# A fused AdaLN block on one core: the experts' second layer as three float32r products, gate rows gathered by GpSimd, all first-layer results on ScalarE

## What is computed

```python
mod = (_silu(L0_c) @ L0_wmod).reshape(L0_c.shape[0], 6, 1, -1)
...
h = _layernorm(x) * (1 + ca) + sa
x = x + ga * attention(h)
h = _layernorm(x) * (1 + cb) + sb
# the experts, on xf = h as 4096 rows of 256
score = softmax(xf @ Wg + bg);  gate, idx = max, argmax        # 16 experts
pos = rank of the token in its expert;  keep = pos < 256
buf[idx, pos] = xf                                             # 16 x 256 rows
hid = relu(einsum('ecd,edh->ech', buf, W1) + b1)               # 256 -> 1024
y = einsum('ech,ehd->ecd', hid, W2) + b2                       # 1024 -> 256
out = where(keep, y[idx, pos] * gate, 0)
x = x + gb * out
```

## Time and profile before

| | us |
|---|---|
| median of 3 runs | 1287.49 (1286.31 to 1287.84) |
| profiled execution, whole | 1285.58 |
| its span, first to last instruction | 1283.7 |
| mean granted TensorE clock | 0.979 of full |

### The profile page before, as it was taken

How to read it: one execution, slowest core, us unless ns; L and a number is a source line. 1 busy time by engine, 2 the same in 40 slices (tenths; PEclk the granted TensorE clock), 3 DMA queues, 4 the chain that set the end, 5 groups by cost and what they waited for, 6 DMA issues and landing times.

```text
span 1283.7 us, 23573 instructions
## 1 busy us (share of the span) xinstructions
PE 1193.8 (93%) x7518; PEld 846.1 (66%) x7518; DVE 860.7 (67%) x2159; ACT 599.7 (47%) x1419; POOL 342.5 (27%) x529
## 2 busy tenths in 40 slices
PE   5799999999999999999999999999998939999995
PEld 2555555656666666666666666666665829999994
DVE  6677777676676766766667666666664546777673
ACT  2465665555555555555555545555444023332320
POOL 3222121213232232323232312224333330111112
PEclk8999999999999999999999999999998959999998
DMA  4520221112121222212121222134425844676730
GB/s 152 203 109 26 107 86 62 37 58 75 59 74 57 74 70 66 84 63 70 65 74 60 73 78 71 59 99 157 162 76 201 305 150 143 200 251 208 239 129 19
DMA packets 100244, 139.66 MB, mean 109 GB/s; under 512 B 9917, under 2 KB 71487, under 8 KB 100033
## 3 DMA queue, kind: packets, MB, share of 16 engines
q1 hardware_dynamic: 91600, 113.55, 26.9%
q10 hardware_dynamic: 4464, 16.25, 3.2%
q0 software_dynamic: 4096, 8.82, 1.8%
HBM read 94.50 MB, written 48.00 MB: 111 GB/s over the span
## 4 chain that ended last, share of the span: by engine, by line
PE 70%; issue 11%; ACT 9%; DVE 6%; POOL 2%; DMA 2%; DVEq 0%; SPq 0%; ACTq 0%; POOLq 0%
PE SC L824 17%; PE Z L844 15%; PE Z L1001 9%; ACT E L1042 8%; PE SC L974 7%; PE XA L880 7%; PE XA L796 3%; PE XB L806 3%; PE XA L806 3%; PE XB L796 2%; PE SC L760 1%; PE XB L866 1%; DVE SC L1344 1%; DVE nm L1344 1%; DMA xln<-in_x 1%
## 5 line engine op out<-in xcount | busy, mean ns | idle before, releaser
L1042 ACT ACTIVATE E<-SC,nm 128x512 f32<-128x512 f32 (+7 forms) x512 | 375.0, 740 | 407.7 <-DVE nm L1344 407.7
L1344 DVE CUSTOM_DVE_ANT_0 SC<-SC,mask 128x512 f32<-128x512 f32 (+7 forms) x512 | 375.9, 786 | 160.3 <-PE SC L824 160.1
L824 PE MATMUL SC<-XQ,XK 64*128 64x512 f32 (+3 forms) x2304 | 264.6, 359 | 32.8 <-ACT E L1042 29.5
L824 PEld LDWEIGHTS SC<-XQ,XK 64*128 64x128 f32 x2304 | 185.5, 186 | 130.6 <-issue 103.3
L844 PE MATMUL Z<-E,vs 128*64 128x512 f32 (+3 forms) x1536 | 270.5, 494 | 0.3 <-DVE vs L1320 0.3
L844 PEld LDWEIGHTS Z<-E,vs 128*64 128x64 f32 x1536 | 99.9, 137 | 135.7 <-issue 124.7
L1001 PE MATMUL Z<-W,hh 128*128 128x256 f32 x512 | 113.2, 379 | 2.3 <-issue 2.3
L1001 PEld LDWEIGHTS Z<-W,hh 128*128 128x128 f32 x512 | 96.0, 190 | 15.1 <-issue 2.7
L1042 ACT ACTIVATION_READ_ACCUMULATOR E<-SC,nm 128x1 f32 x512 | 101.4, 198 | 0.0
L880 PE MATMUL XA<-woT,zt 128*128 128x256 f32 x384 | 89.3, 385 | 0.0
L1133 ACT ACTIVATE hh<-SC,b1t 128x256 f32<-128x256 f32 x64 | 26.9, 471 | 121.1 <-PE SC L974 121.1
(11 more groups left out here) (247 smaller groups left out, 1987.0 us busy)
## 6 DMA issues: line engine op xcount, KB each, us to landing
W<-in_w SPq DMA_DIRECT2D x32, 1024.0 KB, 8.2
z_s<-zs ACTq DMA_DIRECT2D x31, 512.0 KB, 2.6
zt<-z_s SPq DMA_DIRECT2D x24, 512.0 KB, 3.8
W<-in_wqk SPq DMA_DIRECT2D x33, 257.0 KB, 2.7
slots_s<-zt SPq DMA_DIRECT2D x16, 520.0 KB, 3.9
xb<-slots_s SPq DMA_DIRECT2D x16, 520.0 KB, 3.8
Wv<-in_wv SPq DMA_DIRECT2D x17, 256.0 KB, 2.6
xln<-in_x SPq DMA_DIRECT2D x24, 128.0 KB, 2.5
```

The costliest lines, as they stand in the source:

```text
L824: last = pe.matmul(SC[h][:, at:at + z - a], XK[rows, ap, kp, lo:lo + P], XQ[rows, ap, qp, a:z], start=(t == 0), stop=(t == 2))
L1042: act.activation(E[:, h, EOFF[kb]:EOFF[kb + 1]], SC[h][:, at:at + S - lo], ACT.Exp, bias=nm[:, h, kb:kb + 1], scale=-1.0, accum_out=rs[:, ...
L1344: dve.tensor_tensor_reduce(SC[h][:, at:at + S - lo], SC[h][:, at:at + S - lo], mask[:, 0:S - lo], 1.0, BIG, ALU.add, ALU.min, nm[:, h, kb: ...
```

## The change

Five things change, all but the table of memory in the expert stage.

1. The second layer is split like the first. ScalarE's `second_high` copies `W2` to `W2h`, VectorE's `second_low` subtracts to `W2l`; `hh` is copied to `hhh` by ScalarE and subtracted to `hhl` by VectorE. TensorE multiplies three pairs, 48 float32r matmuls in place of 16 float32 ones.
2. ScalarE takes all four groups of the first layer's results; `hh` has one buffer, and ScalarE waits for the last `hhl` (`hh_lo`) before it fills it again.
3. The eight gate operations on VectorE go. GpSimd casts a row number from a new column `MODROW` of the slot rows and gathers the modulation rows for the 256 tokens from DRAM (`mod_s`) into `grow` by two indirect DMAs. VectorE sums the four gate columns (`gsum`) and multiplies by both in one fused operation per half.
4. `W2` has two buffers of its own and a load of its own (`load_second_weights`), which in SyncE's queue waits for `w2_hi` and `w2_lo` of the expert two before.
5. The tiles `modB`, `woT` and `zt` lie lower, so that `hh`, `hhh` and `hhl` can take their place; the new column is filled by a few memsets; some semaphores are merged.

```diff
+MODROW = GATE + B
...
+        top[0] = place["modB"]
+        hh = sb("hh", [P, NM, CAP])
+        hhh = sb("hhh", [P, 2, NM, CAP], F32R)
+        hhl = sb("hhl", [P, 2, NM, CAP], F32R)
+        assert top[0] == place["E"]
...
-        W2 = sb("W2", [P, NW, NM, D])
+        W2 = sb("W2", [P, 2, NM, D])
+        W2h = sb("W2h", [P, 2, NM, D], F32R)
...
+        def load_second_weights(eng, e, k):
+
+            eng.dma_start(W2[:, k % 2, :, :], w2_d[e].rearrange("(m p) n -> p m n", p=P)).then_inc(w2_in[k % 2], 16)
+
         def load_expert(eng, e, k):
 
-            eng.dma_start(W2[:, k, :, :], w2_d[e].rearrange("(m p) n -> p m n", p=P)).then_inc(we_in[k], 16)
...
+                sp.wait_ge(w2_hi, k - 1)
+                sp.wait_ge(w2_lo, k - 1)
+                load_second_weights(sp, k, k)
...
+                    sp.wait_ge(w2_hi, e - 1)
+                    settle(sp, sp_passed)
+                    sp.wait_ge(w2_lo, e - 1)
+                    settle(sp, sp_passed)
+                    load_second_weights(sp, e, k)
...
-                pe.wait_ge(we_in[k], 48 * (j + 1))
                 pe.wait_ge(y_done, e + ONE)
-                for m in range(4):
-                    pe.wait_ge(hid_done[m], e + 1)
+                pe.wait_ge(w2_hi, e + 1)
+                pe.wait_ge(w2_lo, e + 1)
+                pe.wait_ge(hh_hi, e + 1)
+                pe.wait_ge(hh_lo, e + 1)
                 for i in range(2):
                     for m in range(NM):
-                        last = pe.matmul(yps[k % 2][:, i * D:(i + 1) * D], hh[:, k % 2, m, i * P:(i + 1) * P], W2[:, k, m, :],
-                                         start=(m == 0), stop=(m == NM - 1))
+                        for n, (x, w) in enumerate(((hhh, W2h), (hhh, W2l), (hhl, W2h))):
+                            last = pe.matmul(yps[k % 2][:, i * D:(i + 1) * D], x[:, k % 2, m, i * P:(i + 1) * P], w[:, k % 2, m, :],
+                                             start=(m == 0 and n == 0), stop=(m == NM - 1 and n == 2))
                 last.then_inc(y_mm, 1)
...
-            def hidden(e, j, k):
-                act.wait_ge(we_in[k], 48 * (j + 1))
+            def second_high(e, j, k):
+                act.wait_ge(w2_in[k % 2], 16 * (NW // 2 * j + k // 2 + 1))
                 if not isinstance(e, int) or e > 1:
                     act.wait_ge(y_mm, e - 1 + ONE)
-                for m in (0, 2):
+                act.activation(W2h[:, k % 2, :, :], W2[:, k % 2, :, :], ACT.Copy).then_inc(w2_hi, 1)
+
+            def hidden(e, j, k):
+                act.wait_ge(we_in[k], 32 * (j + 1))
+                if not isinstance(e, int) or e > 0:
+                    act.wait_ge(hh_lo, e)
+                if not isinstance(e, int) or e > 1:
+                    act.wait_ge(y_mm, e - 1 + ONE)
+                for m in range(4):
                     act.wait_ge(hid_mm[m], e + 1)
                     for half in range(2):
-                        last = act.activation(hh[:, k % 2, 2 * m + half, :], hid[m][:, half * CAP:(half + 1) * CAP], ACT.Relu,
+                        last = act.activation(hh[:, 2 * m + half, :], hid[m][:, half * CAP:(half + 1) * CAP], ACT.Relu,
                                               bias=b1t[:, k, 2 * m + half:2 * m + half + 1])
                     last.then_inc(hid_done[m], 1)
+                for m in range(4):
+                    act.wait_ge(hid_done[m], e + 1)
+                act.activation(hhh[:, k % 2, :, :], hh[:, :, :], ACT.Copy).then_inc(hh_hi, 1)
 
             def expert(j, k):
                 e = NW * j + k
                 if not isinstance(e, int) or e + 1 < NE:
                     hidden(e + 1, j + (k + 1) // NW, (k + 1) % NW)
+                    second_high(e + 1, j + (k + 1) // NW, (k + 1) % NW)
...
             weights_high(1, 0, 1)
+            second_high(0, 0, 0)
...
-            def hidden(e, j, k):
-                dve.wait_ge(we_in[k], 48 * (j + 1))
+            def second_low(e, k):
+                dve.wait_ge(w2_hi, e + 1)
                 if not isinstance(e, int) or e > 1:
                     dve.wait_ge(y_mm, e - 1 + ONE)
-                for m in (1, 3):
-                    dve.wait_ge(hid_mm[m], e + 1)
-                    for half in range(2):
-                        last = dve.tensor_scalar(hh[:, k % 2, 2 * m + half, :], hid[m][:, half * CAP:(half + 1) * CAP],
-                                                 b1t[:, k, 2 * m + half:2 * m + half + 1], 0.0, ALU.add, ALU.max)
-                    last.then_inc(hid_done[m], 1)
-
-            FIN = 2 * B + 2
+                dve.tensor_tensor(W2l[:, k % 2, :, :], W2[:, k % 2, :, :], W2h[:, k % 2, :, :].bitcast(F32), ALU.subtract).then_inc(w2_lo, 1)
+
+            def hidden(e, k):
+                dve.wait_ge(hh_hi, e + 1)
+                if not isinstance(e, int) or e > 1:
+                    dve.wait_ge(y_mm, e - 1 + ONE)
+                dve.tensor_tensor(hhl[:, k % 2, :, :], hh[:, :, :], hhh[:, k % 2, :, :].bitcast(F32), ALU.subtract).then_inc(hh_lo, 1)
+
+            FIN = 4
 
             def expert(j, k):
                 e = NW * j + k
                 if not isinstance(e, int) or e + 1 < NE:
-                    hidden(e + 1, j + (k + 1) // NW, (k + 1) % NW)
+                    hidden(e + 1, (k + 1) % NW)
+                    second_low(e + 1, (k + 1) % NW)
                 if not isinstance(e, int) or e + 2 < NE:
                     rows_low(e + 2, (k + 2) % NW)
                     weights_low(e + 2, (k + 2) % NW)
 
                 dve.wait_ge(xb_in[k], 16 * (j + 1))
-                for b in range(B):
-                    for i in range(2):
-                        col = xb[:, k, i, GATE + b:GATE + b + 1]
-                        if b == 0:
-                            if not isinstance(e, int) or e > 0:
-                                dve.wait_ge(fin, FIN * e)
-                            last = dve.tensor_scalar(grow[:, i, :], modB[:, b, GB, :], col, None, ALU.mult)
-                        else:
-                            dve.wait_ge(fin, FIN * e + 2 * (b - 1) + i + 1)
-                            last = dve.scalar_tensor_tensor(grow[:, i, :], modB[:, b, GB, :], col, grow[:, i, :],
-                                                            ALU.mult, ALU.add)
-                        last.then_inc(fin, 1)
+                if not isinstance(e, int) or e > 0:
+                    dve.wait_ge(fin, FIN * e)
+                dve.tensor_reduce(gsum[:, :], xb[:, k, :, GATE:GATE + B], AX.X, ALU.add).then_inc(fin, 1)
+                dve.wait_ge(we_in[k], 32 * (j + 1))
                 dve.wait_ge(y_mm, e + 1 + ONE)
                 if not isinstance(e, int) or e > 1:
 
@@ -1647,9 +1689,12 @@
                 rows = yb[:, k % 2, :, :]
                 dve.tensor_tensor(rows, Z[:, (k % 2) * HALF:(k % 2 + 1) * HALF].rearrange("p (i d) -> p i d", i=2),
                                   b2B[:, k, :].unsqueeze(1).broadcast_to([P, 2, D]), ALU.add).then_inc(fin, 1)
-                dve.wait_ge(fin, FIN * e + 2 * B + 1)
-                dve.tensor_tensor(rows, rows, grow[:, :, :], ALU.mult).then_inc(fin, 1)
-                dve.wait_ge(fin, FIN * e + 2 * B + 2)
+                dve.wait_ge(fin, FIN * e + 2)
+                dve.wait_ge(gathered, 32 * (e + 1))
+                for i in range(2):
+                    dve.scalar_tensor_tensor(yb[:, k % 2, i, :], yb[:, k % 2, i, :], gsum[:, i:i + 1], grow[:, i, :],
+                                             ALU.mult, ALU.mult).then_inc(fin, 1)
+                dve.wait_ge(fin, FIN * e + 4)
                 dve.tensor_tensor(rows, rows, xb[:, k, :, D:2 * D], ALU.add).then_inc(y_done, 1)
...
+            second_low(0, 0)
+            hidden(0, 0)
...
+            mod_rows_d = mod_s.rearrange("b (k d) -> (b k) d", d=D)
...
+                pool.tensor_copy(gidx[:, k % 2, :].unsqueeze(2), xb[:, k, :, MODROW:MODROW + 1]).then_inc(tok_ok, 1)
                 pool.tensor_copy(tok[:, k % 2, :].unsqueeze(2), xb[:, k, :, TOKEN:TOKEN + 1]).then_inc(tok_ok, 1)
-                pool.wait_ge(tok_ok, e + 1)
+                pool.wait_ge(tok_ok, 2 * e + 2)
+                settle(pool, pool_passed)
+
+                for i in range(2):
+                    pool.indirect_dma_start(grow[:, i, :], None, mod_rows_d, bass.IndirectOffsetOnAxis(gidx[:, k % 2, i:i + 1], 0),
+                                            bounds_check=6 * B - 1, oob_is_err=False).then_inc(gathered, 16)
```

More of the change, by code:

```diff
@@ L314, in adaln_block @@
         prs = sb("prs", [P, 1])
+        low = ExitStack()
+        modB = sb("modB", [P, B, 6, D], stack=low)
+        woT = sb("woT", [P, PAIRS, D], stack=low)
+        zt = sb("zt", [P, 2, PAIRS, P], stack=low)
         att = ExitStack()
@@ L370, in adaln_block @@
         att.close()
-        top[0] = place["E"]
+        low.close()
+        top[0] = place["modB"]
[3 more added lines that the diff above has]
+        assert top[0] == place["E"]
         xb = sb("xb", [P, NW, 2, ROW])
@@ L387, in adaln_block @@
```

(44 more changed lines are left out.)

10 lines of the change are left out of this document (5 added, 5 removed).

## The result

The changed kernel takes 1362.7 us (median of 4 runs, 1361.4 to 1365.1) against 1286.9: ratio 1.060, 95% interval 1.058 to 1.061.

The account below looks back on a forecast made before the run. TensorE was taken to bound the kernel before; the side engines' order would make it wait. 1285.58 + 50.7 (chain, start, end) + 28 and 0.7 (clock) = 1365.0, 1367 as median; range 1336 to 1385.

Parts of the forecast that it names:

- The chain: Expert stage: TensorE's next first layer waits for VectorE's W1l, 16.5 us per period against 13.1; 44.2 us over 13 periods.
- Rival (b): Expert stage: TensorE stays the bound, so the change is faster, 1273 us; chance 0.05.
- The clock: TensorE's clock falls at restarts after gaps of about 4.2 us: 2.0 us in each of 14, 28 us.
- rival (a): Expert stage: chain as forecast, but TensorE's clock holds in the gaps, 1338 us; chance 0.15.
- The start: Start of expert stage: single-buffered hh makes expert 1's results wait for hhl(0), delaying expert 2 by 5.4 us.
- The end: From expert 15's first layer to the span's end: 1.1 us more, plus 2.0 and 0.7 for the clock.
- the 10.3 us from the last addition's end to the end of the span as before: Tail after the last expert's last addition: taken as unchanged from the kernel before, 10.3 us.
- The gathers: Mid-stage gate-row gathers: landing 2.4 to 7.0 us, cost zero, with 2.2 to 6.8 us of cover.
- Rival (c): Expert stage: the gathers become the wait, 1404 us at a landing of 14 us; chance 0.07.
- Ahead of the stage: Everything before the expert stage: no change, 0 within 1 us either way.
- The total: Whole kernel: median forecast at 1367 us, slower than before.

Follow-up runs that it names:

- warm: Changed kernel with 30 extra float32r matmuls, results unused, after the second layer of each of experts 0 to 13; 1336.3 us.
- w2l_late: Changed kernel with VectorE's subtraction W2l of expert e+1 moved behind bTl and W1l of e+2; 1342.1 us.
- both_late: Changed kernel with VectorE's hhl and W2l both moved behind bTl and W1l of e+2, ScalarE's order untouched; 1346.3 us.
- w2_last: Changed kernel with both W2 steps last: ScalarE copies W2h after bTh and W1h, VectorE subtracts W2l after W1l; 1314.2 us.
- reorder_nogather: The run reorder with gate rows gathered only for expert 0, the other 15 pairs of gathers left out; 1272.0 us.
- decoupled: The run reorder with two buffers and semaphores for gate rows, gathers requested before the wait for the previous finish, and W1 loads issued earlier; 1272.9 us.
- act_all: Kernel before the change with ScalarE taking all four groups of the first layer's results and VectorE none; 1286.0 us.
- after_nogather: Changed kernel with gate rows gathered only for expert 0, the other 15 pairs of gathers left out; 1360.0 us.
- reorder: Changed kernel, same work reordered: ScalarE does W1h of e+2 first, VectorE W1l and bTl of e+2 before hhl and W2l; 1324.7 us.
- thin: The run reorder with VectorE's three subtractions (W1l, W2l, hhl) cut short for experts 2 to 15; 1306.4 us.

## Why the prediction was right, and where it was off

**The chain.** Right in its members, their order and its length: 16.5 counted, 16.35 measured at full clock (warm). The 3.4 us per period became 3.3. w2l_late, both_late and w2_last show that position decides: full-clock periods of 15.4, 15.4 again and 14.16, where 15.5, no change and 14.3 were counted from the same durations, with the same work in all of them. Rival (b), TensorE as the bound, was true of the work and false of the order: reorder_nogather and decoupled reached its 11.95.

**The clock.** Right, and partly by luck: it was the term with the least ground, its size taken from two falls in the kernel before. 2.0 per restart were taken, 1.9 measured (18.23 - 16.35); the 14 first layers of the changed kernel took 7.38 to 8.66 us in the chain where warm's took 5.98 to 6.01. What was wrong is the reading of the earlier trace rows that put gaps of 2.3 and 2.98 on a safe side and rival (a) beside it: at 3.22 us nearly every restart lost clock (w2l_late), at 2.0 three of thirteen (w2_last). The length of a gap alone doesn't say whether it falls. The gap of 2.28 us before the last second layer, which the prediction read in the kernel before, shows it too: act_all has the same gap of 2.28, its clock is at 0.50 from 1264 to 1266 us, and that second layer takes 8.71 us against 7.16. What the prediction cites from the Trainium skill (TensorE: Matmul & The Clock Gate, "HAM oscillation — how this bites in real kernels") agrees with the changed kernel: the loss came anew in each of the 14 restarts. It doesn't hold for every wait in a loop: in w2_last TensorE waits 1.9 to 2.1 us before each of thirteen layers, and ten of them kept the full clock.

**The start.** 5.4 counted, 4.7 measured, the same mechanism: hh as one buffer puts expert 1's results behind hhl(0).

**The end.** Mis-sized: 3.8 counted, 5.9 measured. The path within was right. From expert 15's first matmul y_done(14) came after 17.24 us (1318.89 to 1336.13; 15.95 and the clock's 2.0 counted), the second gather was issued 5.8 after that (5.7 counted) and landed in 3.0 (2.4 counted). Chain of the changed kernel:

```profile
1335.43 0.70 DVE yb L1698
...
1341.91 3.02 DMA grow<-mod_s,gidx
...
1345.94 0.70 DVE yb L1698
...
1348.87 1.00 POOL out L1944
```

The step that failed is "the 10.3 us from the last addition's end to the end of the span as before": they were 13.1 (1346.64 to 1359.7). From the start of the last scatter to the end of the span it is 8.2 us in the kernel before, 8.2 in act_all, 8.4 in both kernels with all but one pair of gathers left out, and 10.8 in the changed kernel and in all seven runs that gather for every expert. So it comes with the gathers, and not with how near the last one is: in decoupled it was issued 18 us before the last scatter. What in them does it is open; the DMA share is 0.00 from 1352 us to the end of the changed kernel's span.

**The gathers.** Cost zero in the periods, right within 0.1 us (after_nogather). Landing 3.0 to 6.4 us, 3.9 in the median, within the bounds 2.4 to 7.0. But the reason for safety was the slow chain itself. Rival (c) priced its landing and took its issue path of 5.7 us as fixed, and that path isn't fixed: it grew to 9.6 in reorder beside VectorE's subtractions.

**Ahead of the stage.** 1.4 us less, just outside the "0 within 1 us either way". No run isolates it: of the ten profiled executions with the new layout nine began expert 0's layer between 1056.4 and 1057.6 and one at 1059.4 (reorder_nogather), the two with the old one at 1057.8 and 1057.9. That is hardly more than their spread, and it is left open.

**The total.** The 4 us between forecast and result are closer than the terms: the periods came 3.4 us shorter than counted, the start 0.7, the stage began 1.4 earlier, and the end was 2.1 longer. Small slips of the prediction changed nothing: of the two dips in the earlier trace rows only the one from 1027 to 1059 us lies between attention and experts (the other is 963 to 995), 35.9 less 34.9 is 1.0 and not 1.1, and the chain's terms as written add up to 16.4 at the end of W1l, not 16.35.

## What to carry to other kernels

Busy shares said that the change pays, and the work alone does pay (decoupled); the order of the queues turned it into a loss of 6%. When a step is put into an in-order queue, count from the instruction that releases the head of that queue to the one that the bounding engine waits for next, and put first what the bounding engine wants first. And after each mended chain price the next loop again with the durations of the new neighbourhood: issue times and landings measured beside idle engines don't hold beside busy ones.

## What the runs showed of the hardware that was not expected

- GpSimd's indirect-DMA issue takes 1.0 us with VectorE idle or short, and 2.2 to 2.9 beside VectorE's 128x2048 float32 subtractions; a cast of 128x2 takes 0.22 against 1.4 (reorder, reorder_nogather, thin, decoupled).
- TensorE's clock fell at restarts after gaps of only 2.0 us in three of thirteen cases, and at 3.22 us in nearly all; after 2.28 us it held once and fell once (the kernel before, act_all); filling a gap with discarded matmuls won 26 us (warm).
- A gather of 128 rows of 1 KB landed in 3.0 us on idle queues and in up to 8.0 where 2 MB of weight loads had been issued just ahead (thin).
- Kernels with a pair of gathers in each expert end 2.5 us later after their last scatter than those without (10.8 against 8.2 to 8.4 us); the cause is open.
